# Attention with a log-sum-exp bounce through DRAM: the bounce moved into the middle of the second pass and onto POOL's DMA queue

## The chip, the cores and the metric

The kernel runs on all 8 cores of one Trainium2 chip. Each core computes one batch element of the input, with the same program and its own copy of the weights; no data passes between cores. The metric is the time of one execution on the device in microseconds (us), that of the slowest core.

## What is computed

The reference is one layer with a residual: attention in chunks and a low-rank feed-forward, both on the same layer-normalised input. Cut to what matters:

```python
xn = layernorm(x)                        # x: 8 x 8192 x 1024
q, k, v = proj(xn, wq, bq), ...          # 16 heads of 64, chunks of 128 tokens
s_intra = q @ k.T * scale                # inside a chunk, 128 x 128 per head
intra = softmax(s_intra) @ v
s_inter = q @ k_means.T * scale          # against the means of this and all earlier chunks
inter = softmax(s_inter) @ v_means
attn = (intra + inter) @ wo.T + bo
ffn = gelu(xn @ U1 @ V1 + b1) @ U2 @ V2 + b2
return x + attn + ffn
```

## The kernel before

The program is written by hand: every instruction is put on one engine's list (`pm.do("t" | "v" | "s" | "y" | "g", ...)`: TensorE, VectorE, ScalarE, SyncE, GpSimd) with the semaphore values that it waits for, and each engine works through its list strictly in order. In the profile these engines are PE, DVE, ACT, SP and POOL. A DMA is on the list of the engine that issues it.

A core goes through its 8192 tokens in 16 super-chunks of 512 tokens. One super-chunk has these stages: transposing of the normalised input, the Q, K and V projections (L420, L439), the means of K (L466) and of V (L482 to L504), the attention for four chunks of 128 tokens (c = 0 to 3), the layer norm of the next super-chunk (L340 to L365), the feed-forward (L808, L830, L838, L854), and the output (L884 to L908).

The attention of a chunk has two passes over the scores, since the softmax is not rescaled afterwards. The first pass (`emit_p1`) computes the scores in six groups: four groups of four heads inside the chunk ("i", L535), and two of eight heads against the means ("n", L563). Each group fills one PSUM bank; ACT takes the exponential (L546, L582), DVE sums it up (L550, L587). Two Ln on ACT (L602, L604) and one operation on DVE (L608) make `neglse`, the negative logarithms of the sums, with 128 tokens on the partitions and 32 columns.

The second pass (`emit_p2_av`) computes the transposed scores and needs these logarithms as rows, laid out along the free dimension. `emit_lse_bounce` brings them there: PE transposes `neglse` into a bank (L616), DVE copies it to `rows_cd` as a high part (L621) and the rest (L624), one DMA writes `rows_cd` to the DRAM buffer `lse_scr` (L631), and when it has landed, five DMAs read it back: one into `fi`, two partitions with the rows of the "i" groups (L634), and four into the partitions of `fb`, one row each, for the "n" groups (L646). The buffers `rows_cd` and `neglse` are single; `lse_scr` and `fi`/`fb` are double (they lie in `H_rot` and `P_fm`).

The second pass then adds the rows to the scores by a matmul with ones (L680) or with a selection matrix (L688), ahead of which or behind which the scores are accumulated into the same bank (L670, L701). The first L680 or L688 of a chunk waits for all five reads (`d_lsl`). ACT takes the exponentials into `A1T` and `A2T` (L712, L718). After the six groups PE multiplies them with V and the means of V (L742, L766) into banks 6 and 7, and DVE copies these to `attn_fm` (L778).

Banks 0 to 5 go round in turn (`pool_next`): six turns for the first pass, six for the second, one for L616.

The order on the lists is that of the emission. Before the change it is: first pass of chunk 0, bounce of chunk 0; then for each chunk c: first pass of c+1, both groups of three and the V matmuls of c, bounce of c+1. On SP's list stand, besides the bounces, the load of the next super-chunk's x (2 MB) and the 64 stores of the output. On POOL's list stand, in the main part, only the copies of the means' rows to `vm_cm` (L501, L504), eight per super-chunk, ahead of the attention.

Of the kernel before, what the change touches and what calls it, by code (L numbers as in the profile page):

```python
# [71 lines left out]
def build_nc(nsc=NSC_FULL, debug=False):  # L72
# [207 lines left out]
    pm = Prog()  # L280
# [37 lines left out]
    sel4_sl = {0: sel4_t[64:68, :], 1: sel4_t[0:4, :]}  # L318
    vrow_slots = {0: A1T[0:1, 0:1024], 1: A2T[0:1, 0:1024]}
    av_done_prev = [0]  # L320
    neglse_guard = [(c_t, 0)]
    attn_guard = (c_v, 0)
    hrot_guard = [(c_t, 0)] * 4
# [49 lines left out]
    for sc in range(nsc):  # L373
# [139 lines left out]
        def pool_next():  # L513
            bk = pool_i[0]
            pool_i[0] = (bk + 1) % 6
            import os
            if os.environ.get("POOL_TRACE"):
                print("pool ->", bk)
            return bk
# [93 lines left out]
        def emit_lse_bounce(cc, neglse_v):  # L613
            bk = pool_next()
            pm.do("t", (lambda bk=bk: lambda e:
                        e.transpose(B[bk][0:32, 0:128], neglse[:], ident[:]))(),  # L616
                  waits=[(c_v, neglse_v), bank_free[bk]], incs=[(c_t, 1)])
            bank_gen[bk] = c_t.n
            neglse_guard[0] = (c_t, c_t.n)
            pm.do("v", (lambda bk=bk: lambda e:  # L620
                        e.tensor_copy(rows_cd[:, 0:128], B[bk][0:32, 0:128]))(),  # L621
                  waits=[(c_t, c_t.n), d_lst], incs=[(c_v, 1)])
            pm.do("v", (lambda bk=bk: lambda e:
                        e.tensor_tensor(rows_cd[:, 128:256], B[bk][0:32, 0:128],  # L624
                                        rows_cd[:, 0:128], ALU.subtract))(),
                  waits=[c_v], incs=[(c_v, 1)])
            rows_v = c_v.n
            bank_free[bk] = (c_v, rows_v)
            scr = lse_scr[cc % 2]
            pm.do("y", (lambda scr=scr: lambda e:  # L630
                        e.dma_start(out=scr, in_=rows_cd[:]))(),  # L631
                  waits=[(c_v, rows_v), lse_guard[cc % 2]], incs=[(d_lst, 16)])
            fi, fb = flat_bufs[cc % 2]
            pm.do("y", (lambda scr=scr, fi=fi: lambda e: e.dma_start(  # L634
                        out=fi.rearrange("two (h t) -> two h t", h=16),
                        in_=scr[0:16, :].rearrange("h (two t) -> two h t",
                                                   two=2)))(),
                  waits=[d_lst, flat_guard[cc % 2], hflat_guard, pq_guard],
                  incs=[(d_lsl, 16)])
            scr5 = scr[16:32, :].rearrange(  # L640
                "(half q2 q4) (two t) -> q2 two half q4 t", half=2, q2=2, two=2)
            for q2i in range(2):
                for twoi in range(2):
                    r = 2 * twoi + q2i
                    pm.do("y", (lambda fb=fb, r=r, scr5=scr5, q2i=q2i,
                                twoi=twoi: lambda e: e.dma_start(  # L646
                                    out=fb[r:r + 1, :].rearrange(
                                        "o (half q4 t) -> o half q4 t",
                                        half=2, q4=4),
                                    in_=scr5[q2i, twoi]))(),  # L650
                          incs=[(d_lsl, 16)])
            return d_lsl.n

        def emit_p2_av(cc, flat_v):
            c = 4 * sc + cc
            ncj = c + 1
            fi, fb = flat_bufs[cc % 2]
            o2 = ones2_sl[cc % 2]
            s4 = sel4_sl[cc % 2]
            exp_done = {}  # L660
            avd = (c_t, av_done_prev[0])
            for kind, g in (("i", 0), ("i", 1), ("n", 0), ("i", 2), ("i", 3),
                            ("n", 1)):
                bk = pool_next()
                if kind == "i":
                    for qi, h in enumerate(grp_heads[g]):
                        base = (h % 2) * 64
                        fc = h // 2
                        pm.do("t", (lambda bk=bk, qi=qi, base=base, fc=fc,
                                    cc=cc: lambda e: e.matmul(  # L670
                                        B[bk][:, qi * 128:(qi + 1) * 128],
                                        k_fm[base:base + 64, fc * 512 + cc * 128:
                                             fc * 512 + cc * 128 + 128],
                                        q_fm[base:base + 64, fc * 512 + cc * 128:
                                             fc * 512 + cc * 128 + 128],
                                        start=(qi == 0), stop=False,
                                        skip_group_check=True))(),
                              waits=([bank_free[bk]] if qi == 0 else ()))
                    pm.do("t", (lambda bk=bk, g=g, fi=fi, o2=o2: lambda e:
                                e.matmul(B[bk][:], o2,  # L680
                                         fi[:, g * 512:(g + 1) * 512],
                                         start=False, stop=True,
                                         skip_group_check=True))(),
                          waits=[(d_lsl, flat_v)], incs=[(c_t, 1)])
                else:
                    par8 = g
                    pm.do("t", (lambda bk=bk, g=g, fb=fb, s4=s4: lambda e:
                                e.matmul(B[bk][:], s4,  # L688
                                         fb[:, g * 512:(g + 1) * 512],
                                         start=True, stop=False,  # L690
                                         skip_group_check=True))(),
                          waits=[bank_free[bk], (d_lsl, flat_v)])
                    hs = [h for h in range(16) if h % 2 == par8]
                    for j, h in enumerate(hs):
                        base = (h % 2) * 64
                        fc = h // 2
                        q8 = cix(h) % 8
                        sl = (q8 % 4) * 128
                        pb = 64 * (q8 // 4)
                        pm.do("t", (lambda bk=bk, sl=sl, pb=pb, base=base,  # L700
                                    fc=fc, cc=cc, ncj=ncj, j=j: lambda e: e.matmul(  # L701
                                        B[bk][pb:pb + ncj, sl:sl + 128],
                                        km_fm[base:base + 64,
                                              fc * 64:fc * 64 + ncj],
                                        q_fm[base:base + 64, fc * 512 + cc * 128:
                                             fc * 512 + cc * 128 + 128],
                                        start=False, stop=(j == 7),
                                        skip_group_check=True))(),
                              incs=([(c_t, 1)] if j == 7 else ()))
                if kind == "i":  # L710
                    pm.do("s", (lambda bk=bk, g=g: lambda e:
                                e.activation(A1T[:, g * 512:(g + 1) * 512],  # L712
                                             B[bk][:], AF.Exp))(),
                          waits=[(c_t, c_t.n), avd] + vm_ready,
                          incs=[(c_s, 1)])
                else:
                    pm.do("s", (lambda bk=bk, g=g: lambda e:
                                e.activation(A2T[:, g * 512:(g + 1) * 512],  # L718
                                             B[bk][:], AF.Exp))(),
                          waits=[(c_t, c_t.n), avd] + vm_ready,  # L720
                          incs=[(c_s, 1)])
                exp_done[(kind, g)] = c_s.n
                bank_free[bk] = (c_s, c_s.n)

            first_in_bank = {}
            av_first = True
            for h in [hh for hh in range(16) if hh % 2 == 0] + \
# [62 lines left out]
        flat_v = {0: fl0}  # L790
        for cc in range(4):
            if cc + 1 < 4:
                nl = emit_p1(cc + 1)
            emit_p2_av(cc, flat_v[cc])
            if cc + 1 < 4:
                flat_v[cc + 1] = emit_lse_bounce(cc + 1, nl)
        a_guard = (c_t, av_done_prev[0])
        attn_done_v = c_v.n
        kq_guard = (c_t, c_t.n)
# [129 lines left out]
    if debug:  # L929
# [11 lines left out]
        for (nm, tt) in dbg_list:  # L941
            od = ap(nc.dram_tensor(nm, list(tt.shape), tt.dtype,
                                   kind="ExternalOutput"))
# [33 lines left out]
```

How the kernel before makes its waits and increments, by code:

```python
            def run(engine):  # L51
                done = {}
                for (ek, waits, fn, incs) in self.steps:
                    if ek != eng_key:
                        continue
                    for (c, val) in waits:
                        if val > 0 and done.get(id(c), -1) < val:
                            engine.wait_ge(c.h, val)
                            done[id(c)] = val
                    instr = fn(engine)
                    for (c, k) in incs:
                        instr.then_inc(c.h, k)
```

## Time and profile before

| | |
|---|---|
| median of the runs (us) | 3791.08 (2 runs: 3651.44 and 3930.72) |
| profiled execution (us) | 3672.33 |
| its span on the slowest core, core 3 (us) | 3670.8 |
| spans of the 8 cores (us) | 3639.6 to 3670.8 |
| granted clock, mean per core | 0.769 to 0.778 |
| PE busy | 2441.7 us, 67% |
| ACT busy | 1208.3 us, 33% |
| DVE busy | 1072.3 us, 29% |
| POOL busy | 85.8 us, 2% |
| SP's DMAs (queue q1) | 26156 packets, 69.35 MB |
| POOL's DMAs (queue q0) | 14592 packets, 13.94 MB |

The first row is a median of only two times that lie 7.6% apart; the profiled execution agrees with the lower one. A super-chunk takes about 220 us. The granted clock is TensorE's, as a share of its full 2.4 GHz. Busy shares are means over stages that have different limits: no engine is near full over the whole span, so what matters is who waits for whom in a stage. In the rows further down a line has the start in us from the span's start, the duration in us, the engine, the line of the kernel, and in brackets how long the engine was idle before and what released it.

### The profile page before, as it was taken

What the parts mean: (1) busy time and instruction counts of PE and PEld (TensorE: products, weight loads), DVE (VectorE), ACT (ScalarE), POOL (GpSimd) and SP (SyncE); (2) the same over time, 40 slices, a digit from 0 to 9 for tenths busy, and PEclk for the clock granted to TensorE, in tenths of its full rate; (3) what the DMA queues carried; (4) which work ended last, traced back from release to release, by engine and by line L of the source; (5) the groups of instructions that cost most, each with busy time, mean ns of one, the idle gap of its engine ahead of it and who ended that gap; (6) DMA issues with size and microseconds to landing.
All of it is one profiled execution on the core that took longest, in us unless ns stands there. A gap on an engine that the chain in (4) does not pass through costs nothing.

```text
span 3670.8 us, 41544 instructions; the slowest of 8 cores (3639.6 to 3670.8 us)
## 1 busy us (share of the span) xinstructions
PE 2441.7 (67%) x14403; PEld 1146.4 (31%) x14403; DVE 1072.3 (29%) x2572; ACT 1208.3 (33%) x2080; POOL 85.8 (2%) x174
## 2 busy tenths in 40 slices
PE   1376857666685776857666685766758576685767
PEld 0233323322332323323322332333323333333333
DVE  2432241323314222142323314232241423224141
ACT  0024133342423324143342423334143332514333
POOL 1100000000000000000000000000000000000000
PEclk9976858678695866959678695877959687695968
DMA  7400101001010000101001010100101000010000
GB/s 117 80 1 2 46 3 46 2 13 35 2 46 3 29 19 2 46 3 47 2 11 37 2 46 3 46 2 2 47 2 46 2 20 27 2 46 2 23 2 24
DMA packets 40951, 85.93 MB, mean 23 GB/s; under 512 B 12428, under 2 KB 19756, under 8 KB 40492
## 3 DMA queue, kind: packets, MB, share of 16 engines
q1 hardware_dynamic: 26156, 69.35, 5.5%
q0 software_dynamic: 14592, 13.94, 2.8%
q8 instruction: 120, 1.97, 0.2%
q14 instruction: 83, 0.68, 0.1%
HBM read 62.03 MB, written 34.60 MB: 26 GB/s over the span
## 4 chain that ended last, share of the span: by engine, by line
PE 56%; DVE 19%; issue 8%; DMA 6%; SPq 4%; ACT 2%; DVEq 1%; ACTq 0%; POOLq 0%
PE B L420 13%; PE B L439 7%; PE B L884 7%; PE B L854 6%; PE B L830 6%; DVE kcol L466 4%; PE B L680 4%; SPq L646 3%; PE B L670 3%; DMA lse_scr<-rows_cd 3%; PE B L742 2%; DVE km_fm L471 2%; DVE out_st L908 2%; DVE stats L340 2%; PE B L701 2%
## 5 line engine op out<-in xcount | busy, mean ns | idle before, releaser
L830 PE MATMUL B<-P_fm,V 128*128 128x512 bf16 x1024 | 322.5, 405 | 202.0 <-DVE P_fm L817 202.0
L838 ACT ACTIVATE H_rot<-B,b_f 128x512 bf16<-128x512 f32 x512 | 348.4, 687 | 90.1 <-PE B L830 89.2
L680 PE MATMUL B<-H_rot,ones 2*128 2x512 bf16 x256 | 153.0, 598 | 325.2 <-DMA P_fm<-lse_scr 186.3
L884 PE MATMUL B<-woT,attn_fm 128*128 128x512 bf16 x1024 | 241.5, 378 | 135.1 <-DVE out_st L908 110.4
L429 ACT ACTIVATE q_fm<-B,bq_eff 128x512 bf16<-128x512 f32 x128 | 88.0, 687 | 730.2 <-PE B L420 730.2
L854 PE MATMUL B<-H_rot,U 128*128 128x512 bf16 x1024 | 307.6, 385 | 9.9 <-ACT H_rot L838 8.9
L453 DVE CAST v_tm<-B 128x512 bf16<-128x512 f32 x128 | 88.5, 692 | 699.7 <-PE B L447 699.7
L420 PE MATMUL B<-xn_fm,wqT 128*128 128x512 bf16 x1024 | 259.5, 421 | 31.9 <-DVE xn_fm L404 31.9
L712 ACT ACTIVATE A1T<-B 128x512 bf16<-128x512 f32 x256 | 152.9, 597 | 301.3 <-PE B L680 301.3
L439 PE MATMUL B<-wvT,xn_fm 128*128 128x512 bf16 x1024 | 252.0, 391 | 0.0
L778 DVE CAST attn_fm<-B 128x512 bf16<-128x512 f32 x128 | 82.5, 686 | 551.9 <-PE B L766 551.9
L420 PE MATMUL B<-xn_fm,wkT 128*128 128x512 bf16 x1024 | 232.6, 390 | 0.0
L830 PEld LDWEIGHTS B<-P_fm,V 128*128 128x128 bf16 x1024 | 103.4, 102 | 340.6 <-issue 236.5
L616 PE MATMUL B<-identity,neglse 128*32 128x128 f32 x64 | 24.8, 388 | 264.2 <-DVE neglse L608 264.2
L908 DVE TENSOR_TENSOR out_st<-B,x_buf 128x512 f32<-128x512 f32 x128 | 88.5, 692 | 374.7 <-PE B L901 371.5
L546 ACT ACTIVATE B<-B,cvals 128x512 f32<-128x512 f32 x256 | 158.1, 657 | 97.6 <-PE B L535 97.4
L884 PEld LDWEIGHTS B<-woT,attn_fm 128*128 128x128 bf16 x1024 | 90.9, 97 | 263.6 <-issue 172.5
L550 DVE TENSOR_REDUCE z<-B 128x4 f32<-128x512 f32 x256 | 164.2, 682 | 19.4 <-ACT B L546 18.0
L870 DVE CAST Q_fm<-B 128x512 bf16<-128x512 f32 x32 | 20.6, 686 | 492.0 <-PE B L854 492.0
L420 PEld LDWEIGHTS B<-xn_fm,wqT 128*128 128x128 bf16 x1024 | 107.6, 106 | 178.5 <-issue 90.6
L466 DVE TENSOR_REDUCE kcol<-k_fm 128x1 f32<-128x128 bf16 x512 | 146.4, 286 | 55.3 <-DVE km_fm L471 3.2
L670 PE MATMUL B<-q_fm,k_fm 64*128 64x128 bf16 x1024 | 153.5, 302 | 6.2 <-DVE z L550 4.6
(102 smaller groups left out, 2825.8 us busy)
## 6 DMA issues: line engine op xcount, KB each, us to landing
x_buf<-L_attn_hidden_states SPq DMA_DIRECT2D x16, 2048.0 KB, 10.4
out<-out_st SPq DMA_DIRECT2D x64, 512.0 KB, 2.7
V<-L_ffn_V POOLq DMA_DIRECT2D x1, 2048.0 KB, 24.5
U<-L_ffn_U POOLq DMA_DIRECT2D x1, 2048.0 KB, 40.1
H_rot<-L_attn_wq POOLq DMA_DIRECT2D x8, 256.0 KB, 4.2
H_rot<-L_attn_wk POOLq DMA_DIRECT2D x8, 256.0 KB, 3.8
H_rot<-L_attn_wv POOLq DMA_DIRECT2D x8, 256.0 KB, 3.9
H_rot<-L_attn_wo POOLq DMA_DIRECT2D x8, 256.0 KB, 3.9
```

Of the source, the lines that this page charges most:

```text
L420: e.matmul(B[bk][:], wT[:, ec * 1024 + fc * 128: ec * 1024 + fc * 128 + 128], xn_fm[:, ec * 512:(ec + 1) * 512], start=(ec == 0), stop=(ec ...
L439: e.matmul(B[bk][:], xn_fm[:, ec * 512 + st * 128: ec * 512 + st * 128 + 128], wvT[:, ec * 1024 + half * 512: ec * 1024 + half * 512 + 512 ...
L466: e.reduce_sum(kcol[:], k_fm[:, fc * 512 + cc * 128: fc * 512 + cc * 128 + 128], axis=AX.X))(),
L546: e.activation(B[bk][:], B[bk][:], AF.Exp, bias=cvals[:, 5:6]))(),
L550: e.reduce_sum(z1[:, 4 * g:4 * g + 4], B[bk][:].rearrange("p (a b) -> p a b", a=4), axis=AX.X))(),
L670: cc=cc: lambda e: e.matmul(B[bk][:, qi * 128:(qi + 1) * 128], k_fm[base:base + 64, fc * 512 + cc * 128: fc * 512 + cc * 128 + 128], q_fm[ ...
L680: e.matmul(B[bk][:], o2, fi[:, g * 512:(g + 1) * 512], start=False, stop=True, skip_group_check=True))(),
L830: pm.do("t", (lambda bk=bk, g=g, rc=rc: lambda e: e.matmul(B[bk][:], V1[:, rc * 4096 + g * 128:rc * 4096 + g * 128 + 128], P_fm[:, rc * 51 ...
L838: pm.do("s", (lambda bk=bk, g=g: lambda e: e.activation(H_rot[:, (g % 4) * 512:(g % 4) * 512 + 512], B[bk][:], AF.Gelu_apprx_tanh, bias=b1 ...
L854: pm.do("t", (lambda gq=gq, rc=rc: lambda e: e.matmul(B[6 + rc][:], U2[:, gq * 256 + rc * 128:gq * 256 + rc * 128 + 128], H_rot[:, (gq % 4 ...
L884: e.matmul(B[bk][:], attn_fm[:, ec * 512 + st * 128: ec * 512 + st * 128 + 128], woT[:, ec * 1024 + half * 512: ec * 1024 + half * 512 + 512],
L908: lambda e: e.tensor_tensor(out_st[:, slot * 1024 + half * 512: slot * 1024 + half * 512 + 512], B[bk][:], xb[:, st * 1024 + half * 512: s ...
```

## The change

Three things are changed. The bounce's six DMAs (L631, L634, L646) are issued by POOL ("g") and no longer by SP ("y"). `emit_p2_av` gets a parameter `part`: 0 emits the first three groups of the second pass ("i" 0, "i" 1, "n" 0), 1 the other three, 2 the V matmuls and the copies to `attn_fm`; the counts of the exponentials are kept in `exp_done_st` across the three calls. And in the loop over the chunks the bounce of chunk c+1 is emitted between part 0 and part 1 of chunk c, where it stood behind the whole of chunk c. The bounce of chunk 0 stays behind the first pass of chunk 0. What is computed is the same.

```diff
--- before.py
+++ after.py
@@ -318,6 +318,7 @@
     sel4_sl = {0: sel4_t[64:68, :], 1: sel4_t[0:4, :]}
     vrow_slots = {0: A1T[0:1, 0:1024], 1: A2T[0:1, 0:1024]}
     av_done_prev = [0]
+    exp_done_st = [{}]
     neglse_guard = [(c_t, 0)]
     attn_guard = (c_v, 0)
     hrot_guard = [(c_t, 0)] * 4
@@ -627,11 +628,11 @@
             rows_v = c_v.n
             bank_free[bk] = (c_v, rows_v)
             scr = lse_scr[cc % 2]
-            pm.do("y", (lambda scr=scr: lambda e:
+            pm.do("g", (lambda scr=scr: lambda e:
                         e.dma_start(out=scr, in_=rows_cd[:]))(),
                   waits=[(c_v, rows_v), lse_guard[cc % 2]], incs=[(d_lst, 16)])
             fi, fb = flat_bufs[cc % 2]
-            pm.do("y", (lambda scr=scr, fi=fi: lambda e: e.dma_start(
+            pm.do("g", (lambda scr=scr, fi=fi: lambda e: e.dma_start(
                         out=fi.rearrange("two (h t) -> two h t", h=16),
                         in_=scr[0:16, :].rearrange("h (two t) -> two h t",
                                                    two=2)))(),
@@ -642,7 +643,7 @@
             for q2i in range(2):
                 for twoi in range(2):
                     r = 2 * twoi + q2i
-                    pm.do("y", (lambda fb=fb, r=r, scr5=scr5, q2i=q2i,
+                    pm.do("g", (lambda fb=fb, r=r, scr5=scr5, q2i=q2i,
                                 twoi=twoi: lambda e: e.dma_start(
                                     out=fb[r:r + 1, :].rearrange(
                                         "o (half q4 t) -> o half q4 t",
@@ -651,16 +652,19 @@
                           incs=[(d_lsl, 16)])
             return d_lsl.n
 
-        def emit_p2_av(cc, flat_v):
+        def emit_p2_av(cc, flat_v, part):
             c = 4 * sc + cc
             ncj = c + 1
             fi, fb = flat_bufs[cc % 2]
             o2 = ones2_sl[cc % 2]
             s4 = sel4_sl[cc % 2]
-            exp_done = {}
+            exp_done = exp_done_st[0]
             avd = (c_t, av_done_prev[0])
-            for kind, g in (("i", 0), ("i", 1), ("n", 0), ("i", 2), ("i", 3),
-                            ("n", 1)):
+            gens = ((("i", 0), ("i", 1), ("n", 0)) if part == 0 else
+                    (("i", 2), ("i", 3), ("n", 1)))
+            if part == 2:
+                gens = ()
+            for kind, g in gens:
                 bk = pool_next()
                 if kind == "i":
                     for qi, h in enumerate(grp_heads[g]):
@@ -722,6 +726,8 @@
                 exp_done[(kind, g)] = c_s.n
                 bank_free[bk] = (c_s, c_s.n)
 
+            if part != 2:
+                return
             first_in_bank = {}
             av_first = True
             for h in [hh for hh in range(16) if hh % 2 == 0] + \
@@ -791,9 +797,12 @@
         for cc in range(4):
             if cc + 1 < 4:
                 nl = emit_p1(cc + 1)
-            emit_p2_av(cc, flat_v[cc])
+            exp_done_st[0] = {}
+            emit_p2_av(cc, flat_v[cc], 0)
             if cc + 1 < 4:
                 flat_v[cc + 1] = emit_lse_bounce(cc + 1, nl)
+            emit_p2_av(cc, flat_v[cc], 1)
+            emit_p2_av(cc, flat_v[cc], 2)
         a_guard = (c_t, av_done_prev[0])
         attn_done_v = c_v.n
         kq_guard = (c_t, c_t.n)
```

## Rows read from the trace of the kernel before

**Rows 1.** The page's first line, and the waits in total: us, times, longest us.
```profile
span 3670.8 us, 41544 instructions; the slowest of 8 cores (3639.6 to 3670.8 us)
...
PE B L680 <- DMA P_fm<-lse_scr: 186.3, 32, 7.4
...
PE B L680 <- DMA H_rot<-lse_scr: 138.9, 32, 4.8
```

**Rows 2.** Stretches, PE: us, busy, clock, DMA, GB/s; attentions 1, 16; one inside.
```profile
257.50:314.50 57.00, 35.92 (x359) 0.50 0.01 3
3546.20:3603.20 57.00, 36.44 (x346) 0.50 0.01 3
1593.10:1602.60 9.50, 9.40 (x99) 0.50 0.01 3
```

**Rows 3.** Order of time, PE, attention of the seventh super-chunk.
```profile
1585.79 0.37 PE L616 MATMUL B<-identity,neglse 128*32 128x128 f32 x1 [16.33 <-DVE neglse L608]
...
1593.05 0.58 PE L680 MATMUL B<-H_rot,ones 2*128 2x512 bf16 x1 [4.07 <-DMA H_rot<-lse_scr]
...
1599.89 0.39 PE L616 MATMUL B<-identity,neglse 128*32 128x128 f32 x1
...
1600.21 1.03 PE L535 MATMUL B<-k_fm,q_fm 64*128 64x128 bf16 x8
...
1602.72 0.58 PE L670 MATMUL B<-q_fm,k_fm 64*128 64x128 bf16 x4 [0.23 <-DVE z L550]
...
1607.69 0.58 PE L680 MATMUL B<-H_rot,ones 2*128 2x512 bf16 x1 [4.38 <-DMA P_fm<-lse_scr]
...
1609.82 0.61 PE L670 MATMUL B<-q_fm,k_fm 64*128 64x128 bf16 x4
...
1614.54 0.39 PE L616 MATMUL B<-identity,neglse 128*32 128x128 f32 x1
...
1629.21 0.39 PE L616 MATMUL B<-identity,neglse 128*32 128x128 f32 x1
...
1637.12 0.58 PE L680 MATMUL B<-H_rot,ones 2*128 2x512 bf16 x1 [6.98 <-DMA P_fm<-lse_scr]
```

**Rows 4.** The same stretch on DVE and SP's queue.
```profile
1586.72 0.28 DVE L624 TENSOR_TENSOR rows_cd<-B,rows_cd 32x128 bf16<-32x128 f32 x1
1587.14 0.33 SPq L631 DMA_DIRECT2D lse_scr<-rows_cd  x1
...
1589.04 2.49 SPq L646 DMA_DIRECT2D H_rot<-lse_scr  x4
...
1600.12 1.29 DVE L778 CAST attn_fm<-B 128x512 bf16<-128x512 f32 x2 [6.96 <-PE B L766]
...
1607.33 0.18 DVE L608 TENSOR_SCALAR neglse<-lnz 128x32 f32<-128x32 f32 x1 [0.68 <-ACT lnz L604]
```

**Rows 5.** Order of time at the start, and one group of POOL's issues (busy us, mean ns).
```profile
3.34 1.73 POOL L192 DMA_DIRECT2D U<-L_ffn_U  x1
...
157.37 0.16 DVE L293 COPY bk_f<-B 128x8 f32<-128x8 f32 x1
158.10 0.55 POOL L192 DMA_DIRECT2D out_st<-L_ffn_b  x1 [5.66 <-DVE bk_f L293]
...
L504 POOL DMA_DIRECT2D vm_cm<-A1T x32 | 15.5, 484 | 0.0
```

**Rows 6.** DMA issues on POOL: count, KB each, median us from issue to landing.
```profile
vm_cm<-A2T POOLq DMA_DIRECT2D x64, 2.0 KB, 1.5
...
out_st<-L_attn_bk POOLq DMA_DIRECT2D x1, 4.0 KB, 4.8
out_st<-L_ffn_b POOLq DMA_DIRECT2D x1, 16.0 KB, 2.3
```

**Rows 7.** Groups by line: busy us, mean ns of one, idle before and its releaser.
```profile
L712 ACT ACTIVATE A1T<-B 128x512 bf16<-128x512 f32 x256 | 152.9, 597 | 301.3 <-PE B L680 301.3
...
L365 DVE TENSOR_SCALAR v_tm<-x_buf,stats 128x1024 bf16<-128x1024 f32 x64 | 52.1, 813 | 56.8 <-ACT stats L361 56.8
```

## The prediction, made before the result was known

> **What bounds the kernel now.** I read the page first: PE 67% busy, DVE 29%, ACT 33%, the 16 DMA engines near nothing outside loads and stores. No engine is full, so the stages have to be read one by one. The waits in total come next: PE loses 325 us in front of the L680 matmuls, in 64 waits, and DMAs that read lse_scr end all of them (186.3 + 138.9, 32 each) [rows 1]. That is one wait per chunk, 20.3 us in each of the 16 super-chunks. The stage around them is the attention: there the granted clock is 0.50 in all 16 super-chunks, the lower of the two levels, 1.2 GHz [rows 2]. I then took one super-chunk near the middle (1580 to 1644 us) in order of time, first PE, then the others [rows 3, 4].
>
> Names: P1(c) is the first pass of chunk c (emit_p1), P2(c) the second with its six groups, T(c) the transposing matmul of L616, bounce(c) the copy to rows_cd, the write to lse_scr and the five loads from it, AV(c) the last matmuls (L742, L766). In rows 3, T(0) stands at 1585.79 and the first L680 of chunk 0 at 1593.05: 7.26 us from T to the first use. T itself, P1(1) and four matmuls of P2(0) fill 3.2 us of that, and PE stands still for the other 4.07. For chunks 1 and 2 the same happens behind AV; for chunk 3 no P1 is left to fill it, and 1629.21 to 1637.12, 7.91 us, holds only four matmuls.
>
> **The change, part by part.** (1) T(c+1) and its bounce move from behind AV(c) to the middle of P2(c). (2) The bounce's six DMAs move from SP's queue to POOL's. (3) P2 is cut into its first three groups (P2a), its last three (P2b) and AV; their order stays. Each chunk still takes 13 turns of the bank pool; T(c+1) now gets the bank of P1(c+1)'s fourth group, which is free before neglse(c+1) can be. No arithmetic is added or removed.
>
> *Price of a bounce on POOL.* No row shows it, so it is built from neighbours. T to the end of the rows copies with DVE free: 1585.79 to 1587.00, 1.2 us [rows 3, 4]. SP picks up 0.14 later; POOL's issue began 0.57 us after the DVE end that released it (157.53 to 158.10) [rows 5]. Write: POOL's one-row copies land 1.5 us after their issue begins [rows 6]; this one goes to DRAM from 32 partitions, I take 1.7. Pickup again: 0.57. Then fi and four row loads, each issue 0.484 as L504's [rows 5], so the last begins 1.95 us after the first. Its landing: 1.5 (vm_cm), 2.3 (b1) or 4.8 (bk, issued just beside a 2 MB load) [rows 6]; the first and second have no competitor, I take 2.2. Sum from T to the first use, call it D: 1.2 + 0.57 + 1.7 + 0.57 + 1.95 + 2.2 = 8.2 us against SP's 7.26. Bounds: with 1.5 and 1.5 D is 7.3; with 4.8 for the load it is 10.8.
>
> The Trainium skill, "DMA: Bandwidth & Descriptors", Specifications, gives about 1 us to the first byte by POOL's path and about 0.6 by SP's. Two legs in a row would then make D about 8.1; by that estimate the sum below would gain 3 us more. It leaves out the pickup, which the rows of this trace show to be larger (0.57 against 0.14), so the sum goes by the rows.
>
> *Chunk 0.* Bounce(0) keeps its place, behind P1(0), with P1(1) as its cover, and PE idle behind that. What is late is therefore paid: 8.2 - 7.26 = 0.94 us lost. T(1) now stands behind P2a(0); neglse(1) is ready some 7.3 us after P1(1) begins (below), near 1593.4, and P2a(0) ends at 1593.05 + 0.94 + 2.13 = 1596.1, so it does not wait, and its own 0.32 us is only moved.
>
> *Chunk 1.* Start from P1(2) on PE (1600.21). Old: the next P1 starts 14.65 later (1614.54 + 0.32). New: P2a(1) may start once P1 is issued and its four score matmuls are through, at +3.05 (1602.72 - 1600.21 + 0.54), and lasts 2.13 (1607.69 to 1609.82), so it ends at +5.2. T(2) then has to wait for neglse(2): its DVE operation ends at +7.30 (1607.33 + 0.18), PE picks up 0.15 later, +7.45. This wait of 2.3 us at the head of PE's queue is new and takes the place of the one that goes; behind it stand P2b(1) and AV(1). The two attn_fm casts are still ahead of the reduces on DVE, the two rows copies no longer, but P1 starts 0.3 earlier against the casts, so I leave the 7.30. T 0.32, P2b and AV 4.72 (1609.82 to 1614.54): 12.49. Saved 2.16. ACT is no bound: P2a's exponentials stand behind the two Ln of P1, which end before neglse's operation starts at +7.12 [rows 4]; three of 0.6 us (L712) [rows 7] end by +8.9, and P2b's first group is ready at +8.9 (T, then two times 0.54).
>
> Is bounce(1) in time? T(1) to the first L680 of chunk 1 has 0.32 + 4.72 + 3.05 = 8.1 us of cover against D = 8.2. The 0.1 is absorbed by the T wait, as is all up to D = 10.4.
>
> *Chunk 2.* Old: 1614.86 to AV(2)'s end at 1629.21, 14.35. New 12.49. Saved 1.86.
>
> *Chunk 3.* Old: 7.91 from AV(2)'s end to its first L680. New: T(3) was issued 5.04 before AV(2)'s end, so 8.2 - 5.04 = 3.16 remain. Saved 4.75. It is no longer hidden, only shorter.
>
> *The rest.* x_buf's load and the out stores stay on SP and lose six predecessors; SP waited for DVE, not the reverse. The vm_cm DMAs on POOL are issued before bounce(0) and after bounce(3) of the previous super-chunk. LN, which follows AV(3), depends on nothing moved and shifts whole. All that costs nothing and gains nothing.
>
> Sum per super-chunk: -0.94 + 2.16 + 1.86 + 4.75 = 7.83 us; times 16: 125 us. The profiled execution took 3672.3 (its span is 3670.8 [rows 1], 1.5 lie around it); 3547 are left of it. The other undisturbed time is 3651.4, and the third, 3930.7, stands 7% above both, so the median of the two runs says little. From 3651 I get 3526; I forecast between them, **3540 us**.
>
> In general a super-chunk saves 24.2 - 2D up to D = 10.4 (each microsecond counts in chunks 0 and 3), and loses 4 for each further one. The low bound D = 7.3 gives 9.6 x 16 = 154 us, so 3497 to 3518; the high one, 10.8, gives 29 us, 3643.
>
> **Rivals.**
>
> *POOL's DMAs land late, no measurable change.* If a small DRAM read by POOL takes 4.8 us as bk's did [rows 6], D is 10.8 and 29 us remain: 3643. Against it: b1's read, four times as large, took 2.3. From D = 9.8 on the gain is under 2%. Chance 0.11.
>
> *POOL's issues are slow, slower than before.* The four row loads have an uneven pattern (half, q4, t), and SP needs 2.49 us for four of them, 0.62 each, against 0.33 for the write [rows 4]: the shape does cost its issuer. POOL's longest issue is 1.73 (U2) [rows 5]. With that for each row load the last begins 5.7 after the first and lands 3.4 later: D = 1.2 + 0.57 + 1.7 + 0.57 + 5.7 + 3.4 = 13.1; the super-chunk loses 4 x 2.7 - 3.4 = 7.4 us, 118 in all: 3790. It decides from D = 11.3 (loss) and 12.4 (over 2%). Against it: U2's issue writes thousands of pieces, a row load eight, and POOL's small ones are all 0.48 to 0.57. Chance 0.05.
>
> *DVE holds POOL up.* The attn_fm casts run at T + 5.3 to 6.6, just where the last three row loads are issued (T + 5.0, 5.5 and 6.0). If they block POOL, the last landings come about 1.1 us later; bounces 1 and 2 absorb it, bounce 3 pays: 17 us, 3564. Against it: these casts read PSUM and take 1.29 us for 2 x 512 columns [rows 4], while L365, from SBUF, takes 0.81 for 1024 [rows 7]; so they are not in the faster mode. The Trainium skill, "SBUF — State Buffer", Who interferes with whom, says that such a lock is taken only in a two-port mode, and that it keeps POOL from writing descriptors. By that rule the term is nothing here. Chance 0.05, same side as the forecast.
>
> *The clock rises.* If PE, with less idle time, were granted 1.00 in the attention, P2b and AV would shrink from 4.72 to about 2.9 (AV halved, P2b held by three exponentials of 0.6), 1.8 per chunk and 115 us more: 3425. Against it: 1593.1 to 1602.6 is already one unbroken stretch of the same matmuls, and it stayed at 0.50 [rows 2]. Chance 0.04.
>
> **How the numbers follow.** Forecast with D from 7.3 to 9.8: 0.75; late landings 0.11; slow issues 0.05; DVE 0.05; clock 0.04. About 2% is what a measurement of this kernel can tell from no change. Faster: 0.75 + 0.05 + 0.04 = 0.84; within 2%: 0.11; slower: 0.05. The range takes in both bounds of D: 3495 to 3645.
>
> **What the profile would show.** PE's wait before L680 for DMAs falls from 325 us to 5.0 + 0.1 + 0.1 + 2.6 per super-chunk, about 125. In front of L616 PE has 32 more waits for neglse (chunks 1 and 2), 2.3 us each, 74 in all. P1 starts lie 12.5 us apart instead of 14.65. L631 starts on POOL about 0.6 us after L624's end, and the row loads follow each other by 0.5. The clock row stays at 0.50 in the attention. The forecast is wrong if D lies over 9.8, if neglse comes later than +7.45, or if that clock moves.

## The result: 3.4% faster, as forecast

| | before | after |
|---|---|---|
| median over all executions (us) | 3669.52 (10) | 3552.22 (11) |
| ratio, after to before | | 0.9661, 95% interval 0.9625 to 0.9697 |
| profiled execution (us), slowest core | 3672.33, core 3 | 3541.88, core 1 |
| PE busy, POOL busy (us) | 2441.7, 85.8 | 2438.2, 298.0 |

In some executions of any of these kernels the cores of one die run at a lower clock and the time is some per cent longer (the profile of e9_t_behind_four below is of such a one); the medians in the first row hold them, while the ratio and every time given below for a kernel leave them out. So taken, the kernel before takes 3648 on the chips of the experiments and the changed one 3525.5 on the chip where it was run again. The forecast was 3540, range 3495 to 3645. By the ratio the gain is 124 us of 3669.5, and side by side in the later run 122; the sum had 125.

The waits before the first L680 (now L684) fell from 325 us [rows 1] to 152. The waits of L617 (the old L616) for `neglse` now number 48 instead of 16. Waits in total, first line before, the others the changed kernel (us, times, longest us):

```profile
PE B L616 <- DVE neglse L608: 264.2, 16, 17.1
...
PE B L617 <- DVE neglse L609: 313.8, 48, 17.0
...
PE B L684 <- DMA H_rot<-lse_scr: 95.2, 32, 5.4
...
PE B L684 <- DMA P_fm<-lse_scr: 56.6, 32, 5.4
```

The seventh super-chunk of the changed kernel on PE, in order of time, against [rows 3]:

```profile
1511.35 0.37 PE L617 MATMUL B<-identity,neglse 128*32 128x128 f32 x1 [16.14 <-DVE neglse L609]
...
1519.71 0.58 PE L684 MATMUL B<-H_rot,ones 2*128 2x512 bf16 x1 [5.17 <-DMA H_rot<-lse_scr]
...
1521.83 0.40 PE L617 MATMUL B<-identity,neglse 128*32 128x128 f32 x1
...
1526.88 1.03 PE L536 MATMUL B<-k_fm,q_fm 64*128 64x128 bf16 x8
...
1530.15 0.58 PE L684 MATMUL B<-H_rot,ones 2*128 2x512 bf16 x1 [0.39 <-DMA P_fm<-lse_scr]
...
1534.11 0.37 PE L617 MATMUL B<-identity,neglse 128*32 128x128 f32 x1 [1.77 <-DVE neglse L609]
...
1539.13 1.03 PE L536 MATMUL B<-k_fm,q_fm 64*128 64x128 bf16 x8
...
1543.30 0.58 PE L684 MATMUL B<-H_rot,ones 2*128 2x512 bf16 x1 [1.28 <-DMA H_rot<-lse_scr]
...
1546.59 0.37 PE L617 MATMUL B<-identity,neglse 128*32 128x128 f32 x1 [1.09 <-DVE neglse L609]
...
1551.61 0.60 PE L674 MATMUL B<-q_fm,k_fm 64*128 64x128 bf16 x4
...
1554.92 0.58 PE L684 MATMUL B<-H_rot,ones 2*128 2x512 bf16 x1 [2.70 <-DMA P_fm<-lse_scr]
```

Every term of the sum can be read here. T to first use (D): 8.36, 8.32, 9.19 and 8.33 us. From T(0) to P1(2): 15.53, where it was 14.42. P1(2) to P1(3), the frame of chunk 1: 12.25, was 14.65. P1(3) to the end of AV(2): 12.48, was 14.35. AV(2)'s end to the first L684 of chunk 3: 3.31, was 7.91. T(2) and T(3) stand behind a wait for DVE, not for a DMA: the wait has changed its kind. The next line is that stretch on PE: us, busy (instructions), granted clock 0.50, DMA share, GB/s. Behind it come DVE and POOL around the first bounce:

```profile
1526.90:1561.70 34.80, 27.42 (x280) 0.50 0.03 4
```

```profile
1512.28 0.28 DVE L625 TENSOR_TENSOR rows_cd<-B,rows_cd 32x128 bf16<-32x128 f32 x1
...
1513.16 0.51 POOL L632 DMA_DIRECT2D lse_scr<-rows_cd  x1 [17.46 <-PE B L564]
1515.61 0.64 POOL L635 DMA_DIRECT2D H_rot<-lse_scr  x1 [1.94 <-DMA lse_scr<-rows_cd]
1516.25 2.16 POOL L647 DMA_DIRECT2D H_rot<-lse_scr  x4
```

And POOL's issues in the changed kernel, count, KB each, median us to landing:

```profile
P_fm<-lse_scr POOLq DMA_DIRECT2D x128, 2.0 KB, 1.8
...
lse_scr<-rows_cd POOLq DMA_DIRECT2D x64, 16.0 KB, 1.7
H_rot<-lse_scr POOLq DMA_DIRECT2D x64, 8.0 KB, 2.1
```

POOL's first issue begins 0.60 us after the DVE operation ends (1512.56 to 1513.16), the write lands in 1.7 (the median of all), POOL needs another 0.75 until the next issue begins (2.45 between the two starts), and the row loads follow each other by 0.54 and land in 1.8.

### The profile page after: what moved, and what is told of

Same layout as the page of the kernel before. It is cut to its first block, busy times and chain, and to the rows that moved or that the text cites. A ratio compares the mean times of both kernels' runs of the same rounds, so it can differ in the third digit from the quotient of the medians.

```text
span 3540.3 us, 41417 instructions; the slowest of 8 cores (3516.9 to 3540.3 us)
## 1 busy us (share of the span) xinstructions
PE 2438.2 (69%) x14403; PEld 1148.5 (32%) x14403; DVE 1078.0 (30%) x2572; ACT 1197.9 (34%) x2080; POOL 298.0 (8%) x558
## 4 chain that ended last, share of the span: by engine, by line
PE 55%; DVE 21%; issue 9%; ACT 4%; DMA 4%; POOL 2%; DVEq 1%; ACTq 0%; POOLq 0%
PE B L421 14%; PE B L893 7%; PE B L440 7%; PE B L863 7%; PE B L839 6%; DVE kcol L467 4%; DVE z L551 3%; PE B L684 3%; DVE km_fm L472 2%; DVE out_st L917 2%; DVE stats L341 2%; PE B L674 2%; PE B L748 2%; DMA lse_scr<-rows_cd 2%; PE B L903 2%
## 5 line engine op out<-in xcount | busy, mean ns | idle before, releaser
L684 PE MATMUL B<-H_rot,ones 2*128 2x512 bf16 x256 | 153.1, 598 | 151.7 <-DMA H_rot<-lse_scr 95.2
L617 PE MATMUL B<-identity,neglse 128*32 128x128 f32 x64 | 24.2, 378 | 313.8 <-DVE neglse L609 313.8
L502 POOL DMA_DIRECT2D vm_cm<-A1T x32 | 16.0, 500 | 2270.5 <-ACT A1T L497 2125.0
```

The costliest lines, as they stand in the source:

```text
L684: e.matmul(B[bk][:], o2, fi[:, g * 512:(g + 1) * 512], start=False, stop=True, skip_group_check=True))(),
```

## The experiments

My theory: the gain is the place of the bounce; POOL's queue takes a part back, about 1 us for each bounce that is exposed; a super-chunk saves 24.2 - 2D while chunks 1 and 2 are absorbed by the wait for `neglse`, and beyond that each microsecond of D counts four times. The rivals are that the queue is part of the gain, and that every bounce is on the path. The second half of the runs asks what is still to be had.

D below is the start of the first L680/L684 of a chunk minus the start of its T, in order of time; a frame is the distance between the starts of two AVs (L742/L748). Both are medians over the 16 super-chunks. P2 is the distance from a chunk's first use to its AV. The last column adds up the time from T(0) to AV(3) over all 16 super-chunks on the profiled core; unlike the medians it holds the bounces that come late. The row of the changed kernel is from c0_changed_again.

| kernel | us | against before | D, chunks 0 / 1 / 2 / 3 | AV to AV 0-1 / 1-2 / 2-3 | P2 of chunk 0 | T(0) to AV(3), sum |
|---|---|---|---|---|---|---|
| before | 3648 | | 7.27 / 7.92 / 7.98 / 7.97 | 14.76 / 14.84 / 14.79 | 4.83 | 907 |
| changed | 3525.5 | -122 | 8.39 / 8.39 / 8.43 / 8.42 | 12.43 / 12.48 / 10.25 | 5.16 | 782 |
| e1_moved_on_sp | 3486.1 | -162 | 7.23 / 7.87 / 7.85 / 7.22 | 12.43 / 12.49 / 9.05 | 5.16 | 744 |
| e2_pool_old_place | 3730.5 | +83 | 8.47 / 9.25 / 9.20 / 9.21 | 16.10 / 16.05 / 16.07 | 4.83 | 991 |
| e3_four_more_dmas | 3612.2 | -36 | 10.37 / 10.37 / 10.43 / 10.74 | 12.61 / 12.83 / 12.55 | 5.16 | 870 |
| e4_eight_more_dmas | 3719.5 | +72 | 12.34 / 12.31 / 12.37 / 12.42 | 14.43 / 14.50 / 14.24 | 5.15 | 977 |
| e5_split_after_five | 3500.5 | -147 | 7.31 / 7.02 / 7.12 / 7.09 | 11.35 / 11.40 / 10.51 | 5.69 | 757 |
| e6_fi_by_itself | 3450.8 | -197 | 4.69 / 7.86 / 7.85 / 5.57 | 12.44 / 12.48 / 8.06 | 6.59 | 710 |
| e7_both | 3444.1 | -204 | 4.79 / 6.26 / 6.24 / 4.77 | 11.00 / 10.98 / 9.50 | 7.05 | 700 |
| e8_i_groups_first | 3409.5 | -239 | 4.78 / 6.25 / 6.24 / 4.67 | 10.83 / 10.88 / 8.66 | 5.70 | 664 |
| e9_t_behind_four | 3429.4 | -219 | 4.80 / 7.34 / 7.31 / 5.07 | 11.91 / 11.96 / 7.98 | 6.22 | 686 |

The differences in the last column are those of the times within 5 us (907 to 782 is 125, where the times differ by 122; 907 to 664 is 243 against 239). So what the kernels gain or lose, they gain or lose in the attention.

### The place alone: the bounce back on SP

```diff
-            pm.do("g", (lambda scr=scr: lambda e:
+            pm.do("y", (lambda scr=scr: lambda e:
...
-            pm.do("g", (lambda scr=scr, fi=fi: lambda e: e.dma_start(
+            pm.do("y", (lambda scr=scr, fi=fi: lambda e: e.dma_start(
...
-                    pm.do("g", (lambda fb=fb, r=r, scr5=scr5, q2i=q2i,
+                    pm.do("y", (lambda fb=fb, r=r, scr5=scr5, q2i=q2i,
```

> The changed kernel, but the bounce's six DMAs are issued by SP again; only the place of the bounce is changed. My theory: the gain comes from the place, and POOL's queue takes part of it back. T to first use (D) is then SP's 7.3 us instead of POOL's 8.3 (8.36, 8.32, 9.19, 8.33 in one super-chunk), and by 24.2 - 2D a super-chunk saves 9.7 us: 155 us less than before, near 3515 where before is 3670, some 35 us under the changed kernel's 3552. Rival: SP's queue was part of the trouble (the bounce stood behind x's load or the stores), so that going back to SP loses; then 3552 or more. The first L684 of chunk 3 should wait about 2.3 us instead of 2.7 to 3.3, and the L617 waits for neglse should stay.

Measured: ratio 0.9539 (0.9479 to 0.96), 3486, 39 us under the changed kernel. D in chunk 0 went from 8.39 to 7.23 and in chunk 3 from 8.42 to 7.22, 2.36 us in a super-chunk, 38 in all: the difference is these two chunks. The frames of chunks 1 and 2 did not move (12.43 and 12.49), since T waits for `neglse` there. The wait before the first L684 of chunk 3 is 1.7 us on the mean, where I had expected 2.3 (a slip: 7.22 less 5.04 of cover and 0.54 of scores is 1.6). The rival, that going back to SP loses, falls. Waits in total:

```profile
PE B L617 <- DVE neglse L609: 330.0, 48, 17.0
...
PE B L684 <- DMA H_rot<-lse_scr: 67.8, 18, 4.7
...
PE B L684 <- DMA P_fm<-lse_scr: 28.3, 19, 2.3
```

The DMA waits number 37 where they were 64, and the wait for `neglse` took up what the DMA waits lost in the chunks between.

### The queue alone: POOL in the old place

The same three lines the other way round, in the kernel before.

> The kernel before, but the bounce's six DMAs are issued by POOL; the place is the old one. My theory: in the old order all four bounces are on the path, so each chunk pays the whole of POOL's extra 1.1 us: 4 x 1.1 x 16 = 70 us slower than before, 3740 where before is 3670 (+1.9%). Rival: the queue was a part of the gain (SP free, issues 0.53 instead of 0.62 us apart); then the time is that of before or less.

Measured: 3730.5, 83 us over before (expected 70). D rose by 1.20, 1.33, 1.22 and 1.24 us, 4.99 in a super-chunk, 80 in all, and the frames by 1.34, 1.21 and 1.28: in the old order every bounce is on the path and pays in full. The DMA waits went from 325 us [rows 1] to 409:

```profile
PE B L680 <- DMA P_fm<-lse_scr: 232.9, 32, 11.1
PE B L680 <- DMA H_rot<-lse_scr: 176.5, 32, 5.9
```

So the queue is no part of the gain. The place brings 162 us, and the queue gives 39 of them back.

### A longer bounce: four and eight more DMAs on POOL

```diff
+            for di in range(4):     # 8 in the second kernel
+                pm.do("g", (lambda di=di: lambda e:
+                            e.dma_start(out=dum_scr[di], in_=rows_cd[:]))(),
+                      incs=[(d_lst, 16)])
             scr5 = scr[16:32, :].rearrange(
```

> The changed kernel with four more DMAs of rows_cd to unused DRAM, issued by POOL between the fi load and the four row loads; they only make the bounce longer, by about 4 x 0.52 = 2.1 us, D = 10.4. My theory (the working behind 24.2 - 2D): the bounces of chunks 1 and 2 stay absorbed by the wait for neglse, those of chunks 0 and 3 pay, 4.2 us in a super-chunk, 67 us over the changed kernel: about 3619. Rival: every bounce is on the path; then 8.4 in a super-chunk, 134 us, 3686. The waits of L617 for neglse in chunks 1 and 2 should fall to near 0 as the waits of L684 grow.

> The same with eight more DMAs, D = 12.5. My theory: the first 2.1 us cost twice, what lies beyond D = 10.4 costs four times: 4.2 + 8.4 = 12.6 us in a super-chunk, 202 us over the changed kernel, about 3754, slower than before by 2%. Rivals: only chunks 0 and 3 ever pay (134 us, 3686), or all four pay from the start (269 us, 3821).

Measured: 3612 (ratio 0.9887, 0.9802 to 0.9973) and 3719.5 (1.0181, 1.0092 to 1.027), 87 and 194 us over the changed kernel; expected 67 and 202, the rivals 134 and 134 or 269. With four more, chunks 0 and 3 pay 2.0 and 2.3 us and the frames of 1 and 2 only 0.18 and 0.35; with the late bounces counted, by the means, it is 2.0, 0.3, 0.5 and 2.8, which is 88 us. Six bounces of chunk 3 are late: POOL began their write 4.2 us after T instead of 1.8, idle with nothing in the profile that it waited for, and that is 13 us or so of the 20 over my sum. With four further ones, each of the four chunks pays 1.7 to 2.0. The knee is real. It lies a little lower than I had put it (10.4), since T is ready at +7.23 (1526.88 to 1534.11) and not +7.45: 3.05 + 2.13 for P2a leaves 2.05 of slack on 8.1 of cover, so near D = 10.1. That holds for the seventh super-chunk; `neglse` becomes ready later from one super-chunk to the next (shown in the section after the experiments), and by the same sum the knee goes from about 9.6 to 10.9. Waits in total, with four, then with eight more:

```profile
POOL lse_scr L634 <- issue: 46.9, 6, 8.1
...
PE B L619 <- DVE neglse L611: 266.6, 25, 17.1
PE B L690 <- DMA H_rot<-lse_scr: 158.6, 32, 7.5
PE B L690 <- DMA P_fm<-lse_scr: 132.4, 32, 8.2
```

```profile
PE B L619 <- DVE neglse L611: 259.4, 16, 17.0
PE B L690 <- DMA H_rot<-lse_scr: 219.5, 32, 9.6
PE B L690 <- DMA P_fm<-lse_scr: 182.9, 32, 8.2
```

Of the 32 waits for `neglse` that the change had brought, 9 are left with four more DMAs, all in the last six super-chunks, where the knee lies higher, and none with eight. The one wait stands in for the other.

### The wait for neglse: T behind the fifth group

From here all kernels have the bounce on SP.

```diff
-            gens = ((("i", 0), ("i", 1), ("n", 0)) if part == 0 else
-                    (("i", 2), ("i", 3), ("n", 1)))
+            gens = ((("i", 0), ("i", 1), ("n", 0), ("i", 2), ("i", 3))
+                    if part == 0 else (("n", 1),))
```

> The bounce on SP (as in e1_moved_on_sp), and placed behind the fifth group of P2 instead of the third, so that T finds neglse ready. What is in dispute: is PE's wait for neglse (1.1 to 1.8 us in chunks 1 and 2 of the changed kernel, up to 2.3 in the run on SP) a loss that can be had back by placing T later? By my bookkeeping hardly. T moves from +7.2 to +7.3, the frame of chunks 1 and 2 would shrink from 12.25 to 10.8, but only 6.5 us then lie between T and the next first use against D = 7.25, so 0.7 comes back as a wait for the DMA (frame 11.6), and in chunk 3 only 3.4 us of cover are left behind T instead of 5.04, which costs 1.65. Per super-chunk 2 x 0.65 - 1.65 = -0.35: 6 us slower than e1_moved_on_sp, that is within 0.5% of its 3486. Rival: the wait for neglse is simply on the path; then 2 x 1.4 x 16 = 45 us are gained, 3441. The waits for neglse should number 16 to 20 instead of 48.

Measured: ratio 0.9606 (0.9581 to 0.9632), 3500.5, 14 us slower than e1_moved_on_sp; expected 6 slower, rival 45 faster. The two kernels ran on different chips, and 14 us is near what such a comparison can tell; the traces say the same (744 to 757). The 32 waits for `neglse` are gone and the frames of chunks 1 and 2 are 1.1 us shorter in the median, but only 0.7 and 0.8 on the mean, since late bounces are no longer absorbed. Against it chunk 3 pays 1.7 on the mean (1.46 in the median) and chunk 0 0.6 (0.5). The frames and chunk 3 came as in my sum (0.65 each, 1.65); chunk 0 was not in it:

```profile
PE B L617 <- DVE neglse L609: 263.8, 16, 17.1
PE B L684 <- DMA H_rot<-lse_scr: 84.5, 32, 5.5
PE B L684 <- DMA P_fm<-lse_scr: 71.4, 32, 5.0
```

So taking the longest new wait away gains nothing while the bounce is what comes next. Where the half microsecond in chunk 0 comes from, e8 shows below.

### fi on a semaphore of its own

```diff
-                  incs=[(d_lsl, 16)])
+                  incs=[(d_lsi, 16)])
...
-                          waits=[(d_lsl, flat_v)], incs=[(c_t, 1)])
+                          waits=[(d_lsi, flat_v[0])], incs=[(c_t, 1)])
...
-                          waits=[bank_free[bk], (d_lsl, flat_v)])
+                          waits=[bank_free[bk], (d_lsl, flat_v[1])])
```

> The bounce on SP in the place of the changed kernel, and the fi load counts on a semaphore of its own: the L684 matmuls wait for fi alone, the L692 matmuls for all loads. The four row loads are issued behind fi and take 2.49 us of SP, so fi lands about 2 us before the last. If what is exposed in chunks 0 and 3 is the tail of the row loads, PE gets it back as far as the two groups in front of the first L692 reach, 1.6 us in chunk 0 and 1.6 of the 2.2 in chunk 3: 3.2 x 16 = 51 us less than 3486, 3435. Rival: the DMAs of a bounce land together, whatever the order of issue; then no change.

Measured: ratio 0.9459 (0.9442 to 0.9475), 3450.8, 35 us less than e1_moved_on_sp; expected 51. The first use in chunk 0 comes 4.69 us after T instead of 7.23, so the loads do not land together and that rival falls. Yet P2 of chunk 0 grew from 5.16 to 6.59: a wait before L693 is the next one. I had taken 1.6 us of cover in front of it; what stands there is one L685 and one group of scores, 1.07, which in two chunks makes 34 us. The term was mis-sized by that.

```profile
PE B L685 <- DMA H_rot<-lse_scr: 28.7, 18, 3.0
PE B L693 <- DMA H_rot<-lse_scr: 13.2, 16, 1.0
PE B L693 <- DMA P_fm<-lse_scr: 2.5, 6, 0.8
```

### Both together

> Both: T behind the fifth group, and fi on its own semaphore. With fi in time (D - 1.9 = 5.35 against 6.5 of cover) the frames of chunks 1 and 2 can shrink to 10.8, so now the wait for neglse is worth something: 2 x 1.4 - 1.65 (chunk 3) = 1.2 us in a super-chunk, 19 us less than e6_fi_by_itself: 3416. Rival: ACT is the next bound (its six exponentials of P2 stand behind the two Ln, and AV waits for them); then no gain over e6_fi_by_itself.

Measured: ratio 0.9452 (0.9425 to 0.9479), 3444.1, 7 us less than e6_fi_by_itself; expected 19, a miss in size. The frames shrank by 1.4 and 1.5, as expected, and chunk 3 gave back 1.44; chunk 0 lost 0.6, which was not in the sum. The row loads also hold up more L693s now (28.5 us in 36 waits, where they were 15.7 in 22). Waits in total, then one of these waits in order of time:

```profile
PE B L693 <- DMA P_fm<-lse_scr: 14.8, 18, 1.3
PE B L693 <- DMA H_rot<-lse_scr: 13.7, 18, 1.0
```

```profile
1487.89 0.60 PE L685 MATMUL B<-H_rot,ones 2*128 2x512 bf16 x1
1489.35 0.58 PE L693 MATMUL B<-H_rot,sel 4*128 4x512 bf16 x1 [0.86 <-DMA H_rot<-lse_scr]
```

ACT as the next bound would have left the frames at 12.4; they are 11.0, so that rival falls.

### The i groups first

The minus lines here and in the last experiment are those of the kernel one experiment earlier.

```diff
-            gens = ((("i", 0), ("i", 1), ("n", 0), ("i", 2), ("i", 3))
+            gens = ((("i", 0), ("i", 1), ("i", 2), ("i", 3), ("n", 0))
                     if part == 0 else (("n", 1),))
```

> As e7_both, with the four i groups in front of both n groups in P2, so that four groups that need only fi cover the row loads. Chunks 0 and 3 each gain what is left of the tail, about 0.3 us: 0.6 x 16 = 10 us less than e7_both, 3406. Rival: as in e7_both, ACT bounds, no gain.

Measured: ratio 0.9347 (0.933 to 0.9364), 3409.5, 35 us less than e7_both; expected 10. I had the tail of the row loads at 0.3 us for a chunk; it was the 28.5 us just shown, and no L693 waits for a DMA any more. An L693 that waited had also lost its place beside the L685 ahead of it, about 0.53 us for each of 36, or 19 us (an estimate from the rows above and below); against both stand 5 us more of waiting for fi and 7 more for `neglse`, and by this count the attention gets 36 shorter, as it does (700 to 664). In order of time, the super-chunk whose T(0) is at 1470.22:

```profile
1478.13 0.60 PE L685 MATMUL B<-H_rot,ones 2*128 2x512 bf16 x1
1478.13 0.60 PE L693 MATMUL B<-H_rot,sel 4*128 4x512 bf16 x1
...
1479.21 0.39 PE L618 MATMUL B<-identity,neglse 128*32 128x128 f32 x1
1479.54 0.60 PE L693 MATMUL B<-H_rot,sel 4*128 4x512 bf16 x1
1480.07 0.61 PE L706 MATMUL B<-q_fm,km_fm 64*25 64x128 bf16 x8
```

This also shows the half microsecond missing in chunk 0 of e5 and e7. The L693 at 1478.13 runs at the same time as an L685, their operands lie on different partitions (0 and 1, and 64 to 67). The one at 1479.54 stands alone behind T and takes 0.53 by itself. Wherever an "n" group does not stand right behind an "i" group, whether T parts them (n 1 in e5 and e7) or another "n" group stands there (here), that is paid once per chunk; in chunk 0 alone it makes 8.5 us over the 16 super-chunks.

### T behind four groups, and two kernels once more

```diff
-            gens = ((("i", 0), ("i", 1), ("i", 2), ("i", 3), ("n", 0))
-                    if part == 0 else (("n", 1),))
+            gens = ((("i", 0), ("i", 1), ("i", 2), ("i", 3))
+                    if part == 0 else (("n", 0), ("n", 1)))
```

Here the row loads also count on one semaphore for each parity of the chunk, since the wait of n 0 now stands behind the next bounce.

> As e8_i_groups_first, with T and the bounce behind the four i groups instead of behind n 0 as well; both n groups follow T, and the row loads get a semaphore for each parity of the chunk. In chunk 3 T has one group more of cover: the first wait for fi there (about 1.3 to 1.8 us) shrinks by 1.07 us. In chunks 1 and 2 T may wait some tenths for neglse; chunk 0 stays, but its n 0 comes no later. By that, 0.3 to 1.07 us in a super-chunk, 5 to 17 us less than e8: 3394 to 3406. Rival: in e8 ACT, not PE, sets the end of chunk 3, so that an earlier T gains nothing.

> e8_i_groups_first once more, as the base of e9: 0.935 of before, 3411.

> The changed kernel once more, on the chip of the two runs that follow, so that they can be compared with it side by side. The same ratio to before as on record, 0.966: about 3525.

Measured on one chip: changed kernel 3525.5 (ratio 0.9666, 0.9638 to 0.9694), e8's kernel again 3406 (0.9336, 0.9309 to 0.9363), T behind four 3429.4 (0.9401, 0.9379 to 0.9422). The last was expected 5 to 17 us faster than e8 and is 23 slower. Chunk 3 gained 0.7 as expected. But the frames of chunks 1 and 2 grew from 10.85 to 11.9: T cannot start before `neglse` is ready, whatever is in front of it, so n 0, moved from before T to behind it, adds its own 1.07 (L693 0.53 and L706 0.54) to the frame. In chunk 0 P2 grew by 0.5, since the L693 of n 0 stands alone there too. The expectation had counted what the earlier T gains in chunk 3 and not what then stands behind it. The attention ran at a granted clock of 0.50, as in all the others.

```profile
1541.12 0.37 PE L618 MATMUL B<-identity,neglse 128*32 128x128 f32 x1 [0.83 <-DVE neglse L610]
```

The kernel of e8, with the bounce on SP, T behind five groups and the i groups first, beats both kernels of the comparison: 6.6% under before, 3.4% under the changed one (3406 against 3525.5, side by side).

## Why the prediction was right, step by step

**The mechanism.** Right. The forecast is the sum of 125 us; 3540 was a middle between what it leaves of two base times. The bounce was on the path in all four chunks [rows 1, 3]; the queue exchanged alone cost 80 us by the D of four chunks, which only fits if all four pay. Moved, it is exposed in chunks 0 and 3 alone, as e3 and e4 show on both sides of the knee.

**The price on POOL.** D was put together as 8.2 and measured at 8.39 to 8.43. The parts, estimate and measurement: pickup 0.57 and 0.60; write 1.7 and 1.7; second pickup 0.57 and 0.75; four issues 1.95 and 2.26 (the fi load's own 0.64 and three of 0.54); last landing 2.2 and 1.8. Two parts were too low by 0.5 together and one too high by 0.4. The estimate from the figures of the Trainium skill, "DMA: Bandwidth & Descriptors", Specifications, came to 8.1; the difference between the queues that it makes, 0.8 us for two legs, was measured as 1.16 (8.39 - 7.23).

**Chunk 0.** Loss 0.94 forecast, 1.11 in the super-chunk shown (15.53 - 14.42).

**Chunks 1 and 2.** 2.16 and 1.86 forecast; 2.40 and 1.87 read there. The wait for `neglse` came as forecast, but shorter in chunk 1: it was ready at +7.09 instead of +7.30, since the copies to `rows_cd` no longer stand on DVE ahead of the reduces. I had seen that and set it against an earlier start of P1, which weighs less. In chunk 2 it came from +7.52 to +7.31, the same 0.21. The D of 9.19 for bounce(2) was absorbed, as everything below the knee is. In total the wait grew by 50 us (264 to 314) and not by the 74 forecast: `neglse` was earlier by that 0.2, and P2a ended later, as D was longer.

One thing the prediction took for granted: that the seventh super-chunk stands for all. In the order before, the frames do not depend on `neglse`; in the new one they do, and `neglse` gets later, since the "n" groups of the first pass run over one more mean with every chunk. Its operation ends 6.57 us after P1(2) starts in the first super-chunk, 7.09 in the seventh and 7.88 in the last, and the frame of chunk 1 grows from 11.7 to 13.1, where before it was about 14.75 with no such growth. From the tenth super-chunk on T starts later than the +7.45 that the prediction named as a sign of being wrong. DVE's reduce in the first and in the last super-chunk of the changed kernel:

```profile
257.36 0.17 DVE L588 TENSOR_REDUCE z<-B 128x8 f32<-128x16 f32 x1 [0.45 <-ACT B L583]
...
3451.39 0.69 DVE L588 TENSOR_REDUCE z<-B 128x8 f32<-128x512 f32 x1 [0.86 <-ACT B L583]
```

Chunk 1 thus saves about 3.0 us in the first super-chunk and 1.7 in the last. The sum came out because the growth is even and the super-chunk that was read lies near the middle, and that part of the hit is luck.

**Chunk 3.** 4.75 forecast, 4.60 read (7.91 - 3.31).

**The sum.** 7.83 forecast; 7.76 in this super-chunk (-1.11 + 2.40 + 1.87 + 4.60), 7.66 on the mean of all (122.5 / 16). The waits before L684 fell to 152 us instead of the 125 that I had named: by chunk they are 5.3, 0.5, 0.7 and 3.0 on the mean, where I had 5.0, 0.1, 0.1 and 2.6. D was 8.4 and not 8.2, and some bounces are late: D reached 9.7 in chunk 2 and 11.05 in chunk 3 at most. In that last one POOL's second issue began 4.9 us after the first instead of 2.3, with nothing in the profile that it waited for; why is not shown. What such waits add in chunks 1 and 2 comes off the wait for `neglse` behind them, and so the time hardly moved.

**The rivals.** Late landings: the small reads took 1.8 us, not 4.8; the bk load still took 5.3 beside the 2 MB load, so that figure is not what a small read on POOL's queue takes as a rule; that the big load is its cause is likely, but no run separates the two. Slow issues: a row load costs POOL 0.54, less than SP's 0.62. DVE in POOL's way: the row loads of bounces 1 to 3 are issued near the `attn_fm` casts, that of bounce 0 is not, and their D is the same (8.39 against 8.39 to 8.43). POOL issued the four row loads in 2.15 us beside the casts and in 2.16 without. With these casts, which read PSUM, the rule of the Trainium skill, "SBUF — State Buffer", Who interferes with whom, agrees; a DVE operation in a two-port mode beside a bounce was not tried. The clock: it stayed at 0.50.

## What to carry to other kernels

When a round trip of DMAs is waited for, place its start where its operands become ready, and count the cover from there to the first use; a microsecond added to the trip costs only where that cover is used up, so the same microsecond cost once per bounce in the old order and, up to about two of them, in two of four chunks in the new. A chain of two dependent small DMAs is paid in pickup, issue and landing; here that made the queues differ by 1.2 us with 2 to 16 KB a piece. What is needed first should be waited for by itself. After such a move look for the operand that now sets the time of the moved instruction: work that fits in front of it until the operand is ready is free, work behind it is not. And read more than one repetition of a loop, the first and the last too, when a length in it depends on the index.

## What the runs showed of the hardware

- POOL reacts more slowly than SP. Its issue began 0.60 us after the DVE operation that released it and 0.75 after its own write had landed, where SP took 0.14 after DVE [rows 4], and began the next issue 1.59 us after the start of a write that lands in 1.4 (1587.14 to 1588.73 in the trace of before). The same write landed in 1.7 against 1.4. From T to the first use POOL took 1.16 to 1.33 us more for a write and the reads that depend on it (by the D of e1 and e2).
- A read of 2 KB from DRAM by POOL landed in 1.8 us (median of 256), one of 8 KB in 2.1; a single one of 4 KB beside a 2 MB load took 5.3.
- Two matmuls with 2 and 4 rows, their operands on different partitions, ran at the same time; parted from each other, the second took 0.53 us of its own.
- The granted clock stayed at its lower level, 1.2 GHz, through long busy stretches of the attention. In e8's kernel 29.3 of 29.8 us were busy at 0.50, with 64 rows or fewer for most of the matmuls. The feed-forward behind it begins at 1512.72 with 128-row matmuls (L818), and from 1514 to 1520 the mean was 0.82:

```profile
1474.90:1504.70 29.80, 29.27 (x277) 0.50 0.02 5
...
1514.00:1520.00 6.00, 4.04 (x14) 0.82 0.00 0
```

Why the clock does not rise there is not shown by these runs; no kernel was made that changes the rows of these matmuls alone.
